# Six matmuls without a use in each batch of the channel attention

## The chip, the cores and the metric

The kernel runs on one core of a Trainium2 chip. The metric is the device time of one execution in microseconds (us), from the start of the program to its end; less is better.

## The reference

Four stages are added one after another to `x` (16 batches of 64 tokens with 256 channels): a gated attention, a mixture of experts, a channel attention and a gated MLP with four-bit weights. The change touches the third:

```python
def _L1_xattn_ref(q, k, v, gamma):
    # q = layernorm(x), k = v = ctx_2048, each (16, 64, 256)
    qh = q.reshape(B, 8, 8, 256); kh = k.reshape(B, 8, 8, 256); vh = v.reshape(B, 8, 8, 256)
    qk = jnp.einsum('bhdq,bhdl->bhql', qh, kh) * scale
    sm = jax.nn.softmax(qk, axis=-1)
    ret = jnp.einsum('bhql,bhdl->bhdq', sm, vh)
    return gamma * ret.reshape(B, Dv, Lq)
x = x + jnp.tanh(g_xattn[1]) * _L1_xattn_ref(...)
```

So in each of the 16 batches 8 heads attend from 256 channels to 256 channels, with only 8 numbers per head and channel in the product.

## The kernel before, in words

`build` (L1693 on) puts the four stages one behind the other. In `channel_attention` each batch passes over the engines like this. TensorE's orders are written out by hand in one loop over the batches, and semaphores tie the engines together.

- `replicate` (L1450): two matmuls of 128 rows and 128 columns against the constant `spread` lay a batch's rows (`split`, the normed x) and its context (`c_split`) out so that heads stand in strips of 32 rows. ScalarE copies the result to `qk_rows` (L1553).
- `row_scores` (L1465), four pairs of heads for a batch: four matmuls each that use 32 rows of the array. VectorE takes the maxima of a pair (L1620) into `context_mx`.
- `turn_maxima` (L1473): two transposes of the maxima; VectorE copies them to `mT` (L1626).
- `column_scores` (L1485, L1490), four pairs: two matmuls over 512 columns that subtract the maxima and four that add the scores, all on 32 rows. They wait for a free bank of three, which ScalarE's exponents (L1561, two for a pair) release.
- `weigh` (L1506): eight float32 matmuls, which the profile lists as sixteen, on strips of 32 output columns; called twice for a batch, with heads 0 to 3 and heads 4 to 7. They write columns 0 to 255 of the bank `OUT_BANK`. When the second is done VectorE takes the values out (L1630), inverts, scales and adds them to x.

The loop works one batch ahead. For batch b it runs, in this order: `replicate(b+2)`, row scores 1 of batch b+1, column scores 0 of batch b, row scores 2 of b+1, column scores 1 of b, the second weighing of batch b-1, row scores 3 of b+1, column scores 2 of b, `replicate(b+2)`, the first weighing of b, the turned maxima of b+1, row scores 0 of b+2, column scores 3 of b. Two weighings thus stand close together, and a long piece of the loop, from the turned maxima to the next weighing, holds none. Ahead of the loop `keep_busy` (L52) runs matmuls of the identity in the same bank `OUT_BANK`.

Of the kernel before, what the change touches and what calls it, by code (L numbers as in the profile page):

```python
# [26 lines left out]
BATCH, SEQ, HID = 16, 64, 256  # L27
# [21 lines left out]
def keep_busy(nc, k, bank, count):  # L49

    for _ in range(count):
        nc.tensor.matmul(k.ps[:, bank, :].rearrange("p (r n) -> p r n", r=4), k.ident[:],  # L52
                         k.ident[:].unsqueeze(1).broadcast_to([P, 4, P]), start=True, stop=True)
# [1318 lines left out]
def channel_attention(nc, k, a):  # L1372
# [5 lines left out]
    x, ident, vec, ps = k.x, k.ident, k.vec, k.ps  # L1378
    k.late_stack = ExitStack()
    k.ffn = FourBitWeights(nc, k, a, k.late_stack)  # L1380
    with ExitStack() as st:
# [8 lines left out]
        c_split, cT = k.context.split, k.context.turned  # L1390
        spread, minus, mx, vmask = k.context.spread, k.context.minus, k.context.mx, k.context.vmask
# [11 lines left out]
        A_BANK, B_BANK, OUT_BANK = 0, 4, 7  # L1403
# [5 lines left out]
        def a_use(b, what):  # L1409
            return (PAIRS + 1) * b + what  # L1410
# [15 lines left out]
        def cut(head):  # L1426
            group, j = divmod(head, C_GROUP)
            return group, slice(C_ROWS * j, C_ROWS * j + C_ROWS)

        @block.sync  # L1430
        def _(sp):

            k.ffn.load(sp, 0, 0)
            k.ffn.load(sp, 0, 1)

        @block.tensor
        def _(pe):
            mm = nc.tensor.matmul

            def replicate(b, group):  # L1440
                n = b_use["rows", b, group]
                if n >= 3:

                    pe.wait_ge(s["b_taken"], n - 2)
                if 2 <= b < 2 * FIRST_TILES and group == 0:
                    pe.wait_ge(s["h_low"], b // 2 * 2 + 2)
                elif b >= 2 * FIRST_TILES and group == 0:
                    pe.wait_ge(s["rest_low"], 2)
                for which, src in enumerate((split, c_split)):
                    last = mm(ps[:, B_BANK + n % 3, which * HID:which * HID + HID], spread[:, 2 * group + which, :], src[:, b, :],  # L1450
                              start=True, stop=True)
                last.then_inc(s["b_ready"], 1)

            def row_scores(b, pair):
                n = a_use(b, pair)
                if pair % 2 == 0:

                    pe.wait_ge(s["b_taken"], b_use["rows", b, pair // 2] + 1)
                if n >= 2:

                    pe.wait_ge(s["a_taken"], n - 1)
                for qt in range(CH):
                    for e in range(2):
                        group, rows = cut(2 * pair + e)
                        last = mm(ps[:, A_BANK + 2 * (n % 2) + e, qt * HID:qt * HID + HID], qk_rows[rows, b % 3, group, 0, qt * P:qt * P + P],  # L1465
                                  qk_rows[rows, b % 3, group, 1, :], start=True, stop=True)
                last.then_inc(s["a_ready"], 1)

            def turn_maxima(b):
                n = a_use(b, TURN)  # L1470
                pe.wait_ge(s["a_taken"], n)
                for qt in range(CH):
                    last = nc.tensor.transpose(ps[:, A_BANK + 2 * (n % 2), qt * P:qt * P + P], mx[:, qt, :], ident[:])  # L1473
                last.then_inc(s["a_ready"], 1)

            def column_scores(b, pair):
                n = b_use["head", b, 2 * pair]
                if pair == 0:

                    pe.wait_ge(s["a_taken"], a_use(b, TURN) + 1)  # L1480

                pe.wait_ge(s["b_taken"], n - 1)
                for e in range(2):
                    group, rows = cut(2 * pair + e)
                    mm(ps[:, B_BANK + (n + e) % 3, :].rearrange("p (c n) -> p c n", c=CH), minus[rows, group, :],  # L1485
                       mT[rows, b % 2, :].unsqueeze(1).broadcast_to([C_ROWS, CH, HID]), start=True, stop=False)
                for c in range(CH):
                    for e in range(2):
                        group, rows = cut(2 * pair + e)
                        last = mm(ps[:, B_BANK + (n + e) % 3, c * HID:c * HID + HID], qk_rows[rows, b % 3, group, 1, c * P:c * P + P],  # L1490
                                  qk_rows[rows, b % 3, group, 0, :], start=False, stop=(c == CH - 1))
                        if c == CH - 1:
                            last.then_inc(s["b_ready"], 1)

            def weigh(b, turn):

                pe.wait_ge(s["b_taken"], b_use["head", b, 4 * turn + 3] + 1)
                if turn == 0:
                    pe.wait_ge(s["values_set"], b + 1)
                    if b > 0:  # L1500

                        pe.wait_ge(s["out_taken"], b)
                for c in range(CH):
                    for quarter in range(4):
                        t, e = divmod(quarter, 2)
                        last = mm(ps[32 * quarter:32 * quarter + 32, OUT_BANK, 0:HID], vmask[:, b % 2, c, 2 * turn + t + 4 * e, :],  # L1506
                                  probs[:, 4 * turn + quarter, c * HID:c * HID + HID],
                                  start=(turn == 0 and c == 0), stop=(turn == 1 and c == CH - 1))
                last.then_inc(s["pv_done"], 1)

            keep_busy(nc, k, OUT_BANK, 5)
            pe.wait_ge(s["h_low"], 2)
            replicate(0, 0)
            replicate(0, 1)
            row_scores(0, 0)
            replicate(1, 0)
            row_scores(0, 1)
            replicate(1, 1)
            for pair in range(2, PAIRS):
                row_scores(0, pair)  # L1520
                keep_busy(nc, k, OUT_BANK, 1)
            turn_maxima(0)
            row_scores(1, 0)
            for b in range(BATCH):
                if b + 2 < BATCH:
                    replicate(b + 2, 0)
                if b + 1 < BATCH:
                    row_scores(b + 1, 1)
                column_scores(b, 0)
                if b + 1 < BATCH:  # L1530
                    row_scores(b + 1, 2)
                column_scores(b, 1)
                if b > 0:
                    weigh(b - 1, 1)
                if b + 1 < BATCH:
                    row_scores(b + 1, 3)
                column_scores(b, 2)
                if b + 2 < BATCH:
                    replicate(b + 2, 1)
                weigh(b, 0)  # L1540
                if b + 1 < BATCH:
                    turn_maxima(b + 1)
                if b + 2 < BATCH:
                    row_scores(b + 2, 0)
                column_scores(b, 3)
            weigh(BATCH - 1, 1)

        @block.scalar
# [240 lines left out]
```

## Time and profile before

| what | us |
|---|---|
| median of three runs | 1049.33 |
| lowest and highest of the three | 1041.99 and 1057.7 |
| the profiled execution, its own time | 1057.21 |
| span of the profiled execution, first to last instruction | 1055.4 |

The profiled execution lies close to the slowest of the three runs; 1.8 us of its time lie outside its span. "PE" is TensorE's matmuls, "PEld" its weight loads, DVE is VectorE, ACT ScalarE, POOL GpSimd. "PEclk" is the granted TensorE clock: 1.00 is 2.4 GHz, 0.50 is 1.2 GHz, and a figure between is a mean over a stretch that has some of both.

### The profile page before, as it was taken

What the parts mean: (1) busy time and instruction counts of PE and PEld (TensorE: products, weight loads), DVE (VectorE), ACT (ScalarE), POOL (GpSimd) and SP (SyncE); (2) the same over time, 40 slices, a digit from 0 to 9 for tenths busy, and PEclk for the clock granted to TensorE, in tenths of its full rate; (3) what the DMA queues carried; (4) which work ended last, traced back from release to release, by engine and by line L of the source; (5) the groups of instructions that cost most, each with busy time, mean ns of one, the idle gap of its engine ahead of it and who ended that gap; (6) DMA issues with size and microseconds to landing.
All of it is one profiled execution on the core that took longest, in us unless ns stands there. A gap on an engine that the chain in (4) does not pass through costs nothing. (4 is left out here: it accounts for less than half of the span.)

```text
span 1055.4 us, 18475 instructions
## 1 busy us (share of the span) xinstructions
PE 927.1 (88%) x6890; PEld 748.7 (71%) x6892; DVE 739.1 (70%) x1240; ACT 564.4 (53%) x1713; POOL 275.9 (26%) x413
## 2 busy tenths in 40 slices
PE   1679999999999999667999999988999996899997
PEld 1678888888888889545777777764555553577776
DVE  7778898988989897665544444456777668657653
ACT  5667787877788877314333333323455544333332
POOL 1133333344333334112322222203011013123130
PEclk9989999999999999887999999996676668999999
DMA  3101010110101000024111110001000000010001
GB/s 143 41 1 61 2 61 2 62 42 21 61 1 61 2 22 2 1 82 154 48 48 48 48 48 3 0 0 60 1 2 2 1 1 30 32 61 30 30 0 40
DMA packets 10929, 35.74 MB, mean 34 GB/s; under 512 B 1248, under 2 KB 5344, under 8 KB 8544
## 3 DMA queue, kind: packets, MB, share of 16 engines
q1 hardware_dynamic: 10704, 34.64, 9.3%
q8 instruction: 49, 0.80, 0.3%
q14 instruction: 32, 0.26, 0.1%
q10 hardware_dynamic: 144, 0.03, 0.0%
HBM read 33.62 MB, written 1.05 MB: 33 GB/s over the span
## 5 line engine op out<-in xcount | busy, mean ns | idle before, releaser
L223 PE MATMUL ps<-wt_hi,xq 128*128 128x256 f32 (+1 forms) x512 | 125.5, 281 | 20.8 <-DVE ctx_lo L727 15.0
L223 PE MATMUL ps<-wt_lo,xq 128*128 128x256 f32 (+1 forms) x512 | 125.2, 285 | 0.0
L223 PEld LDWEIGHTS ps<-wt_hi,xq 128*128 128x128 f32 x512 | 101.0, 197 | 23.8 <-DVE ctx_lo L727 15.4
L370 ACT ACTIVATE square<-ps 128x128 bf16<-128x128 f32 x384 | 100.9, 295 | 27.8 <-PE ps L223 27.8
L1561 ACT ACTIVATE ca_probs<-ps 128x512 f32<-128x512 f32 x128 | 69.5, 595 | 71.2 <-PE ps L1490 71.2
L223 PEld LDWEIGHTS ps<-wt_lo,xq 128*128 128x128 f32 x512 | 100.8, 197 | 0.0
L1138 POOL TENSOR_TENSOR moe_w_lo<-moe_w_all,moe_w_hi 128x384 fp32r<-128x384 f32 x48 | 52.8, 1133 | 141.6 <-ACT moe_w_hi L1241 141.6
L517 POOL TENSOR_TENSOR rstd<-rstd,half_neg 128x6 f32<-128x6 f32 x64 | 88.3, 1380 | 5.0
L370 ACT ACTIVATION_READ_ACCUMULATOR square<-ps 128x1 f32 x384 | 85.9, 226 | 0.0
L1620 DVE TENSOR_REDUCE context_mx<-ps 128x4 f32<-128x1024 f32 x64 | 76.9, 1223 | 12.0 <-PE ps L1465 11.3
L1305 DVE TENSOR_TENSOR moe_act_g<-moe_act_g,ps 128x512 f32<-128x512 f32 x48 | 33.1, 690 | 71.6 <-PE ps L1175 71.6
L1257 ACT CAST moe_in_hi<-moe_inner 128x512 fp32r<-128x512 f32 x48 | 29.8, 621 | 94.6 <-DVE moe_inner L1308 83.0
L391 ACT ACTIVATE kT<-ps,vec 128x128 f32<-128x128 f32 x128 | 51.7, 458 | 49.2 <-PE ps L235 49.2
L294 PE MATMUL ps<-wp_hi,catq 128*128 128x256 f32 x256 | 66.9, 299 | 11.7 <-DVE catq L101 11.7
L1175 PE MATMUL ps<-moe_hT_hi,moe_w_hi 128*128 128x512 f32 x192 | 76.9, 400 | 0.0
L1175 PE MATMUL ps<-moe_hT_hi,moe_w_lo 128*128 128x512 f32 x192 | 76.4, 398 | 0.0
L1175 PE MATMUL ps<-moe_hT_lo,moe_w_hi 128*128 128x512 f32 x192 | 76.2, 397 | 0.0
L522 POOL TENSOR_TENSOR probs<-probs,total 128x512 f32<-128x512 f32 x32 | 35.2, 1099 | 154.2 <-DVE total L632 154.2
L232 PE MATMUL ps<-ident,qn 128*128 128x128 f32 x256 | 42.4, 290 | 27.4 <-DVE qn L601 27.4
L597 DVE TENSOR_TENSOR qn<-ps,rstd 128x512 f32<-128x512 f32 x64 | 44.1, 689 | 30.5 <-POOL rstd L517 30.4
L294 PE MATMUL ps<-wp_lo,catq 128*128 128x256 f32 x256 | 65.2, 292 | 0.0
L294 PEld LDWEIGHTS ps<-wp_hi,catq 128*128 128x128 f32 x256 | 51.5, 201 | 14.9 <-DVE catq L101 14.9
(211 smaller groups left out, 2602.8 us busy)
## 6 DMA issues: line engine op xcount, KB each, us to landing
moe_w_all<-in_experts SPq DMA_DIRECT2D x8, 1152.0 KB, 5.3
w_in<-in_wt SPq DMA_DIRECT2D x8, 1024.0 KB, 5.9
wp_in<-in_wp SPq DMA_DIRECT2D x8, 512.0 KB, 3.6
ffn_codes<-in_codes SPq DMA_DIRECT2D x8, 384.0 KB, 3.1
ffn_w_scales<-in_code_scales SPq DMA_DIRECT2D x8, 384.0 KB, 3.7
x_rows<-in_x SPq DMA_DIRECT2D x2, 512.0 KB, 4.6
ctx_in<-in_ctxT SPq DMA_DIRECT2D x1, 1024.0 KB, 9.3
context_rows<-in_ctx SPq DMA_DIRECT2D x1, 1024.0 KB, 9.8
```

The source lines that it names most:

```text
L223: last = mm(ps[:, first + bank, col:col + width], left[:, c, tokens], w[:, c, wcol:wcol + width], start=(j == 0), stop=(j == len(steps) - 1))
L232: last = nc.tensor.transpose(ps[:, bank, j * P:j * P + P], qn[:, i % 2, j, :], ident[:])
L294: last = mm(ps[:, CAT_BANK + j, q * HID:q * HID + HID], catq[:, f // HPG, f % HPG, t * P:t * P + P], w[:, f, :], start=(n == 0), stop=(n = ...
L370: last = nc.scalar.activation(square[:, i % 2, j, :], ps[:, bank, (j % 4) * P:(j % 4) * P + P], ACT.Square, scale=float(HD) ** -0.5, accum ...
L391: last = nc.scalar.activation(kT[:, r, t * P:t * P + P], ps[:, PROJ + 2 * (i % 2) + 1, r * P:r * P + P], ACT.Identity, bias=vec[:, V_HLN + ...
L517: nc.gpsimd.tensor_tensor(rstd[:, i % 2, :], rstd[:, i % 2, :], k.half_neg[:, 0:6], ALU.pow).then_inc(s["rstd_ready"], 1)
L522: nc.gpsimd.tensor_tensor(probs[:, r], probs[:, r], total[:, r, :].unsqueeze(2).broadcast_to([P, 8, SEQ]), ALU.mult).then_inc(s["probs_rea ...
L597: nc.vector.tensor_tensor(qn[:, i % 2, 0:4, :], ps[:, bank, :].rearrange("p (h d) -> p h d", h=4), rstd[:, i % 2, 0:4].unsqueeze(2).broadc ...
L1138: last = nc.gpsimd.tensor_tensor(w_lo[:, b, cols], w_all[:, b, cols], w_hi[:, b, cols].bitcast(F32), ALU.subtract)
L1175: last = mm(ps[:, bank, :], w[:, b, col:col + P], h[:, c, tokens], start=(n == 0), stop=(n == len(steps) - 1))
L1561: nc.scalar.activation(probs[:, head, :], ps[:, B_BANK + n % 3, :], ACT.Exp, scale=float(C_DIM) ** -0.5).then_inc(s["b_taken"], 1)
L1620: nc.vector.tensor_reduce(dst, ps[:, bank:bank + 2, :].rearrange("p e (q l) -> p e q l", q=CH), AX.X, ALU.max).then_inc(s["a_taken"], 1)
```

## The change

TensorE gets a helper `spare()` with two matmuls of 128 rows, 128 columns and 256 columns of moving data. Their operands are constant by then (`spread`, and the context of batches 0 and 1), they write columns 256 to 511 of `OUT_BANK`, which nothing reads, and they neither wait for a semaphore nor raise one. It is called in each of the 16 passes of the loop at three places: ahead of column scores 0, ahead of column scores 1, and behind column scores 1.

```diff
+            def spare():
+
+                for b in range(2):
+                    mm(ps[:, OUT_BANK, HID:2 * HID], spread[:, 0, :], c_split[:, b, :], start=False, stop=False, skip_group_check=True)
+
...
                 if b + 1 < BATCH:
                     row_scores(b + 1, 1)
+                spare()
                 column_scores(b, 0)
                 if b + 1 < BATCH:
                     row_scores(b + 1, 2)
+                spare()
                 column_scores(b, 1)
+                spare()
                 if b > 0:
                     weigh(b - 1, 1)
```

TensorE's matmuls of one pass before, from the second `replicate` matmul's end up to the second weighing (L1465 row scores, L1485 and L1490 column scores, L1506 weighing):

```order
 L1465 MATMUL ps<-ca_qk_rows 128x256 x4
-L1485 MATMUL ps<-ca_mT,context_minus 128x512 x2
-L1490 MATMUL ps<-ca_qk_rows 128x256 x4
-L1465 MATMUL ps<-ca_qk_rows 128x256 x4
-L1485 MATMUL ps<-ca_mT,context_minus 128x512 x2
-L1490 MATMUL ps<-ca_qk_rows 128x256 x4
-L1506 MATMUL ps<-ca_probs,context_vmask 32x256 x8
```

And the same piece of the changed kernel (L1498 is the new helper, and the weighing's line is now L1511):

```order
+L1498 MATMUL ps<-context_split,context_spread 128x256 x2
+L1485 MATMUL ps<-ca_mT,context_minus 128x512 x2
+L1490 MATMUL ps<-ca_qk_rows 128x256 x4
+L1465 MATMUL ps<-ca_qk_rows 128x256 x4
+L1498 MATMUL ps<-context_split,context_spread 128x256 x2
+L1485 MATMUL ps<-ca_mT,context_minus 128x512 x2
+L1490 MATMUL ps<-ca_qk_rows 128x256 x4
+L1498 MATMUL ps<-context_split,context_spread 128x256 x2
+L1511 MATMUL ps<-ca_probs,context_vmask 32x256 x8
```

Nothing changes its place against anything else; three pairs of matmuls are put in between. The other engines run the same instructions in the same order.

## Rows read from the trace of the kernel before

**Rows 1.** The page: its first line, and the granted clock in 40 slices.

```profile
span 1055.4 us, 18475 instructions
PEclk9989999999999999887999999996676668999999
```

**Rows 2.** Windows: the loop of the channel attention, and the stage behind it.

```profile
core 0: us, PE busy (x) PEld busy (x) DVE busy (x) ACT busy (x) POOL busy (x), PEclk, DMA share, GB/s
727.93:886.70 158.77, 145.98 (x1225) 85.60 (x1223) 111.92 (x165) 84.27 (x157) 17.49 (x114) 0.70 0.01 1
886.70:1055.40 168.70, 148.00 (x619) 113.89 (x620) 99.19 (x138) 55.03 (x81) 41.55 (x35) 0.96 0.10 35
```

**Rows 3.** Windows from one batch's turned maxima to the next; first, last two, three between.

```profile
727.93:738.24 10.31, 9.06 (x58) 5.68 (x56) 5.23 (x5) 5.60 (x9) 0.00 (x0) 0.50 0.01 2
...
770.73:778.26 7.53, 6.70 (x82) 4.17 (x79) 5.99 (x9) 5.06 (x10) 1.16 (x8) 1.00 0.01 2
778.26:787.71 9.45, 8.94 (x82) 4.99 (x78) 7.70 (x13) 5.54 (x11) 1.16 (x8) 0.77 0.01 2
787.71:799.47 11.76, 11.53 (x82) 6.80 (x78) 7.18 (x10) 5.30 (x10) 1.16 (x8) 0.50 0.00 0
...
870.24:877.00 6.76, 5.90 (x78) 3.66 (x74) 5.96 (x9) 4.53 (x9) 1.16 (x8) 1.00 0.00 1
877.00:886.70 9.70, 7.05 (x80) 4.00 (x80) 8.02 (x23) 5.47 (x11) 1.20 (x2) 1.00 0.01 2
```

**Rows 4.** Windows: four stretches of the loop that end where the clock changes.

```profile
769.70:783.40 13.70, 12.36 (x145) 7.63 (x144) 12.06 (x19) 9.54 (x20) 1.16 (x8) 1.00 0.01 2
783.40:800.40 17.00, 16.77 (x120) 9.34 (x116) 9.98 (x17) 7.34 (x14) 2.32 (x16) 0.50 0.00 0
800.40:803.80 3.40, 2.58 (x28) 1.87 (x26) 3.37 (x5) 2.39 (x5) 0.00 (x0) 1.00 0.02 5
803.80:807.20 3.40, 3.40 (x30) 1.71 (x32) 1.13 (x2) 1.35 (x3) 0.56 (x5) 0.51 0.00 0
```

**Rows 5.** Timeline of TensorE in the batch at clock 1.00: start, us, instruction, idle before.

```profile
772.20 0.50 PE L1465 MATMUL ps<-ca_qk_rows 32*128 32x256 f32 x4
773.11 0.49 PE L1485 MATMUL ps<-ca_mT,context_minus 32*128 32x512 f32 x2 [0.41 <-ACT ca_probs L1561]
...
774.49 0.50 PE L1485 MATMUL ps<-ca_mT,context_minus 32*128 32x512 f32 x2 [0.42 <-ACT ca_probs L1561]
...
775.15 1.07 PE L1506 MATMUL ps<-ca_probs,context_vmask 128*32 128x256 f32 x16
...
776.83 0.39 PE L1450 MATMUL ps<-ca_split,context_spread 128*128 128x256 f32 x1
777.05 0.28 PE L1450 MATMUL ps<-context_split,context_spread 128*128 128x256 f32 x1
777.26 1.07 PE L1506 MATMUL ps<-ca_probs,context_vmask 128*32 128x256 f32 x16
```

**Rows 6.** Timeline of TensorE in the batch at clock 0.50.

```profile
789.49 0.58 PE L1450 MATMUL ps<-ca_split,context_spread 128*128 128x256 f32 x1
789.87 0.41 PE L1450 MATMUL ps<-context_split,context_spread 128*128 128x256 f32 x1
790.22 0.79 PE L1465 MATMUL ps<-ca_qk_rows 32*128 32x256 f32 x4
...
792.70 0.79 PE L1485 MATMUL ps<-ca_mT,context_minus 32*128 32x512 f32 x2 [0.23 <-ACT ca_probs L1561]
...
793.85 1.94 PE L1506 MATMUL ps<-ca_probs,context_vmask 128*32 128x256 f32 x16
```

**Rows 7.** Timeline of TensorE ahead of the loop: full-array matmuls in a row at clock 1.00.

```profile
719.64 0.28 PE L1450 MATMUL ps<-context_split,context_spread 128*128 128x256 f32 x1
719.76 0.28 PE L1450 MATMUL ps<-ca_split,context_spread 128*128 128x256 f32 x1
```

**Rows 8.** Timeline of TensorE: waits in the first pass, and in the last.

```profile
732.59 0.80 PE L1485 MATMUL ps<-ca_mT,context_minus 32*128 32x512 f32 x2 [1.00 <-ACT ca_probs L1561]
...
734.50 0.79 PE L1485 MATMUL ps<-ca_mT,context_minus 32*128 32x512 f32 x2 [0.25 <-ACT ca_probs L1561]
...
885.58 1.07 PE L1506 MATMUL ps<-ca_probs,context_vmask 128*32 128x256 f32 x16 [1.17 <-ACT ca_probs L1561]
```

## The prediction

> **What bounds the kernel now.** I read the page first: its line of granted clocks is 8 or 9 tenths nearly everywhere, but 6 or 7 in five of six slices near the end of the third quarter [rows 1]. The windows view puts them in the loop of the channel attention: 158.77 us at a mean clock of 0.70, against 0.96 in the stage behind it [rows 2]. TensorE is busy 145.98 us of those 158.77, the next engine (VectorE) 111.92. So the loop is bound by TensorE, and its clock counts in full.
>
> Then I cut the loop at each batch's turned maxima. The same 82 matmuls take 7.53 us at clock 1.00 and 11.76 us at 0.50; a batch with some of both takes 9.45 us [rows 3]. That is the price of the clock: up to 4.23 us a batch. From the first turned maxima (727.93) to those of batch 14 (870.24) the loop needs 142.31 us for 14 passes; the last 13 take (870.24 - 738.24)/13 = 10.15 us each. On the scale from 7.53 to 11.76 they are (10.15 - 7.53)/4.23 = 62% at the lower level.
>
> Last I looked at what TensorE does before the clock changes. It goes down to 0.50 at 783.4 and 803.8 [rows 4]. Both times the piece without a weighing has just passed: score matmuls on 32 rows of the array, with waits of about 0.4 us for ScalarE [rows 5]; the next weighing has just begun or is about to. The clock comes up at 769.7, 800.4 and 807.2, when replicate matmuls, a weighing and often the turned maxima have just run. It is the same in the other spells of the loop. So I read this: the piece without a weighing does too little to hold 2.4 GHz, and the change puts full-array matmuls (128*128) just there.
>
> By the Trainium skill ("TensorE: Matmul & The Clock Gate", table of what matters for a kernel, "avoid throughput drops mid-kernel") the clock drops when there are idle gaps of microseconds between bursts of matmuls. The trace does not agree: the gaps before the fall at 783.4 are no longer than about 0.4 us. By that rule the new matmuls would cure nothing and only cost: that is the second rival below.
>
> **The change, part by part.** Nothing is removed or moved, no wait is added; nobody waits for the new matmuls but what stands behind them on TensorE.
>
> - *Price of one pair at 1.00.* A pair of replicate matmuls has the same shape and tile: 776.83 to 777.26 is 0.43 us [rows 5]. In a row without a stop one takes 0.12 us [rows 7], a pair 0.24. I take 0.43, since each pair stands among matmuls with other weights, as the replicate pair does. Bounds 0.24 and 0.43.
> - *Price of one pair at 0.50.* 789.49 to 790.22, 0.73 us [rows 6]; twice the lower bound, 0.48, is the other end.
> - *Places 1 and 2 at 1.00* lie in front of two waits for ScalarE's exponents, 0.41 and 0.42 us [rows 5]. The pair fills them and is free to within 0.02 us. Without that cover each costs 0.43.
> - *Place 3 at 1.00* stands before a weighing that does not wait [rows 5]: 0.43 us. So a batch at 1.00 takes 7.53 + 0.43 = 7.96 us. VectorE has 5.99 and 7.70 us of work in neighbouring batches [rows 3] and stays below that on the mean.
> - *A batch at 0.50* has cover only at place 2, 0.23 us [rows 6]: 11.76 + 3 x 0.73 - 0.23 = 13.72 us, that is 1.96 us more.
> - *The first pass* (10.31 us, all at 0.50) has waits of 1.00 and 0.25 us at places 1 and 2 [rows 3, 8]: 0 + 0.48 + 0.73 = 1.21, so 11.52 us.
> - *Behind batch 14* the clock is 1.00 in both kernels, and the last weighing waits 1.17 us for ScalarE anyway [rows 3, 8]: at most 0.43 for the pass of batch 14. I take 0.4.
> - *The bank.* The pairs write the bank that VectorE reads (L1630), other columns of it. No row shows what that costs; between 0 and 0.43 us a batch (VectorE waiting out one pair). I take 0, since the read starts after the weighing, with no pair beside it at 1.00.
>
> *The sum.* The clock is low when the loop starts, as before, and the new pairs do not raise it: it must first meet a stretch of weighing and replicating at the right moment. I take the first pass at 0.50 and the second half and half, (13.72 + 7.96)/2 = 10.84 us, then twelve at 1.00: 12 x 7.96 = 95.5 us. Together 11.52 + 10.84 + 95.5 = 117.9 us against 142.3: 24.4 less. With 0.4 at the end the gain is 24.0 us. The profiled execution's 1057.2 would become 1033.2 (span 1031.4). It lies 7.9 us above the median; the excess I put down to clock spells elsewhere, such as slices 17 to 19 [rows 1], which this does not touch. From the median 1049.3 I get 1025.3 us, 2.3% less.
>
> **The rivals.**
>
> 1. *Stuck at 1.2 GHz (ends slower).* A pair takes 0.73 us at the lower level and so stretches the very batches that are slow. If the clock does not come up, a batch costs 13.72 us. With n such batches after the first and the rest at 7.96 the loop takes 11.52 + 13.72n + 7.96(13 - n) + 0.4 = 115.4 + 5.76n. It equals 142.3 at n = 4.7, is 2% slower (21 us) at 8.3, and with n = 13 the kernel takes 1049.3 + 48 = 1097 us. For it: before, the clock stayed low for 17.0 us at a stretch [rows 4], 1.4 batches; the new batches are longer and their mixture at the lower level no denser (matmul busy 11.53 of 11.76 us already [rows 3]). Against it: every spell before ended within about one and a half batches, by replicate, weighing and turning, which all remain. Before, the alignment between batches and clock changes moved on from spell to spell; if longer batches repeat at the same alignment, all 13 can miss. Runs would then differ much. Chance 0.19; 1051 to 1097, middle 1074.
> 2. *The pairs cost but do not hold the clock.* By the mix before, (0.62 x 1.96 + 0.38 x 0.43) = 1.38 us in each of 13 batches, with 1.2 and 0.4 at the ends 19.5: 1069 us. For it: the skill's rule above, and that the first pass stays at 0.50 throughout although identity matmuls run ahead of it. Against it: nothing else but the kind of matmul distinguishes stretches that hold the clock from those that lose it. Chance 0.13.
> 3. *It holds, but not always.* The clock falls two more times, as once three batches were 9.45, 11.76 and about 9.2 us. Each fall costs some 5 us: 1035 us. For it: one pair at 1.00 adds only 0.43 us of full-array work to a piece that lasts from 778.3 to 782.7. Chance 0.16.
>
> **How the numbers follow.** Forecast 0.52, rivals 0.19, 0.13, 0.16. The forecast's own range: 14 passes with only the first at 0.50 and pairs at 0.34 (between the two bounds) give 11.5 + 13 x 7.87 = 113.8, 28 less, 1021; a full second batch at 0.50 gives 1028. The three runs lie 7 to 8 us around their median, so a median of three can be off by some 4: 1017 is the low end. The high end takes in rivals 3 and 2 and the better half of 1: 1069. About 2% (21 us, 1028.3) is what a measurement of this kernel can tell from no change. Faster by more: most of the forecast, a little of rival 3, 0.49. Slower by more (over 1070): 0.17, from rival 1 and the upper side of 2. Within: 0.34.
>
> **What would show it.** In the changed kernel's profile: granted clock near 0.95 in the loop instead of 0.70; batches of about 8.0 us from turn to turn; the waits for ScalarE at places 1 and 2 gone, with the new line's pairs in their stead; each pair 0.43 us to the next matmul; a spell at 0.50 only at the loop's start. Wrong, if batches at 1.00 take over 8.3 us (cover misjudged), if the clock falls in the piece with the pairs (rival 2 or 3), or if a spell at 0.50 outlasts two batches (rival 1).

## The result and the profile after

| | before | changed |
|---|---|---|
| median of 20 executions, us | 1055.84 | 1052.12 |
| lowest and highest, us | 1041.05, 1060.15 | 1031.50, 1107.77 |
| profiled execution, its own time and span, us | 1057.21, 1055.4 | 1091.61, 1089.8 |
| mean granted clock of the profiled span | 0.921 | 0.886 |

The comparison of the two gives 0.9877 (95% interval 0.9834 to 0.992), so 1.2% less; it leaves out the executions that lie more than 1.5% above the fastest of their kernel. In the changed kernel that is where the story is: they are ten of the 20, and the medians of all 20 differ by 0.4% only. With the runs called same_again and third_sample, which are the changed kernel once more, there are 36 executions, and they lie in three groups with nothing between them: 18 from 1031.5 to 1041.3 us, 10 from 1062.7 to 1068.8, and 8 from 1091.6 to 1107.8. Over all 36 the median is 1052.0. The kernel before spreads from 1041 to 1062 us in all its runs, without such gaps.

The profile after fell into the third group. The first line of its page and the granted clock in 40 slices, to be read against [rows 1]:

```profile
span 1089.8 us, 18669 instructions
PEclk8789999999999998888999999975555587899999
```

Where there were sixes there are now fives. The windows view, from turned maxima to turned maxima, in the columns of [rows 3]; last, the whole spell at the lower level:

```profile
core 0: us, PE busy (x) PEld busy (x) DVE busy (x) ACT busy (x) POOL busy (x), PEclk, DMA share, GB/s
728.65:740.06 11.41, 11.41 (x64) 7.27 (x62) 5.33 (x5) 5.60 (x9) 0.00 (x0) 0.50 0.01 1
740.06:753.80 13.74, 13.74 (x88) 8.24 (x84) 10.13 (x11) 5.30 (x10) 1.21 (x8) 0.50 0.00 1
753.80:767.55 13.75, 13.75 (x88) 8.25 (x85) 7.17 (x10) 5.30 (x10) 1.15 (x8) 0.50 0.00 1
...
863.78:877.52 13.74, 13.74 (x88) 8.24 (x84) 7.17 (x10) 5.30 (x10) 1.15 (x8) 0.50 0.00 0
877.52:886.30 8.78, 8.76 (x88) 5.51 (x85) 6.36 (x9) 5.07 (x10) 1.15 (x8) 0.89 0.01 2
886.30:894.27 7.97, 7.97 (x88) 5.08 (x84) 6.37 (x10) 5.30 (x11) 1.15 (x8) 1.00 0.01 2
894.27:902.42 8.15, 8.15 (x89) 5.11 (x85) 7.09 (x12) 5.29 (x11) 1.15 (x8) 1.00 0.00 0
...
722.40:879.40 157.00, 157.00 (x933) 93.66 (x931) 84.43 (x113) 59.60 (x111) 12.96 (x81) 0.50 0.00 1
```

TensorE is busy in every microsecond of 157 us and its clock stays at 1.2 GHz. Behind the first pass, ten follow each other at 13.74 or 13.75 us. In the next the clock comes up (8.78 us), and two passes of 7.97 and 8.15 us follow. From the first turned maxima to those of batch 14 the loop takes 902.42 - 728.65 = 173.8 us against 142.3 before: 31.5 of the 34.4 us that the profiled execution is slower. Of the rest 0.7 us had been lost before the loop (it starts at 728.65, not 727.93), and the remaining 2.2 come behind batch 14.

TensorE's timeline of one low pass, as in [rows 6] (L1498 is the new pair; the weighing is L1511 here):

```profile
838.79 0.79 PE L1465 MATMUL ps<-ca_qk_rows 32*128 32x256 f32 x4
839.51 0.80 PE L1498 MATMUL ps<-context_split,context_spread 128*128 128x256 f32 x2
840.24 0.79 PE L1485 MATMUL ps<-ca_mT,context_minus 32*128 32x512 f32 x2
...
841.81 0.80 PE L1498 MATMUL ps<-context_split,context_spread 128*128 128x256 f32 x2
842.54 0.79 PE L1485 MATMUL ps<-ca_mT,context_minus 32*128 32x512 f32 x2
...
843.69 0.80 PE L1498 MATMUL ps<-context_split,context_spread 128*128 128x256 f32 x2
844.41 1.94 PE L1511 MATMUL ps<-ca_probs,context_vmask 128*32 128x256 f32 x16
```

Each pair takes 0.72 or 0.73 us to the next matmul. And of a pass at 2.4 GHz, as in [rows 5]:

```profile
887.77 0.50 PE L1465 MATMUL ps<-ca_qk_rows 32*128 32x256 f32 x4
888.20 0.51 PE L1498 MATMUL ps<-context_split,context_spread 128*128 128x256 f32 x2
888.67 0.50 PE L1485 MATMUL ps<-ca_mT,context_minus 32*128 32x512 f32 x2
...
889.58 0.50 PE L1498 MATMUL ps<-context_split,context_spread 128*128 128x256 f32 x2
890.06 0.50 PE L1485 MATMUL ps<-ca_mT,context_minus 32*128 32x512 f32 x2
...
890.73 0.50 PE L1498 MATMUL ps<-context_split,context_spread 128*128 128x256 f32 x2
891.16 1.07 PE L1511 MATMUL ps<-ca_probs,context_vmask 128*32 128x256 f32 x16
```

The waits of 0.41 and 0.42 us for ScalarE are gone, filled by pairs of 0.47 and 0.48 us, and the third pair adds its 0.43 us in front of the weighing. This is a pass of 7.97 us.

### The profile page after: what moved, and what is told of

It is laid out like the page before. It is cut to its first block and busy times, and to the rows that moved or that the text cites. A ratio compares the mean times of both kernels' runs of the same rounds, so it can differ in the third digit from the quotient of the medians.

```text
span 1089.8 us, 18669 instructions
## 1 busy us (share of the span) xinstructions
PE 974.2 (89%) x6988; PEld 779.4 (72%) x6988; DVE 739.9 (68%) x1240; ACT 563.7 (52%) x1713; POOL 275.6 (25%) x413
```

## The experiments

The theories, as the expectations name them. A: the pairs hold the higher clock once it is there, but a low pass keeps in step with the moments at which the clock can change, so a low spell can last. B: the pairs only cost. C: any matmul in the waits would do. D: the third pair is needed. E: the more work at the low level, the longer it stays low. F: the start decides everything.

**The changed kernel again: same_again and third_sample.** No edit.

> The changed kernel once more, to see more executions and, if the profile falls on one, an execution that runs well. Theory A (the pairs hold the higher clock once it is there, but a pass at the lower level takes 13.75 us and repeats at nearly the same place against the moments at which the clock can change, so that a low spell can last for many passes): executions lie in clusters, some at 1031 to 1041 us and some at 1063 to 1108; passes at clock 1.00 take 7.97 us, with no fall inside the loop. Theory B (the pairs only cost, the clock moves as before): all executions near 1070 us, the clock goes up and down within the loop at passes of 8 to 13.7 us.

> The changed kernel a third time, for a profile of an execution that runs well (both profiles so far fell on executions near 1100 us). If the profile falls on one near 1032 to 1041: one low spell at the loop's start, passes of 7.97 and 8.15 us, and, as in the run called kick, a short fall of the clock in about one pass of four, 9.6 to 9.7 us. If it falls on the middle cluster (1063 to 1069): a low spell of 6 or 7 passes of 13.75 us, then the same.

Eight executions of the first: 1032.1, 1033.1, 1033.8, 1062.7, 1065.4, 1066.1, 1100.2, 1101.4 us. Eight of the second: five from 1031.8 to 1034.2, then 1066.7, 1067.7 and 1093.6. The groups are those of the first 20, so theory B, which has no groups, falls. Both profiled executions belong to the third group, with low spells that run through the first 13 and 12 passes. Behind the first pass of 11.40 us they are again of 13.74 and 13.75 us each. TensorE was busy throughout; the whole spell of same_again, and that of third_sample:

```profile
721.00:905.20 184.20, 184.20 (x1099) 109.92 (x1097) 98.28 (x133) 70.04 (x131) 15.74 (x98) 0.50 0.00 1
720.40:891.00 170.60, 170.60 (x1017) 101.75 (x1013) 90.95 (x122) 64.82 (x121) 14.55 (x90) 0.50 0.00 1
```

The pass at 1.00 that follows in third_sample is of 8.16 us; the one of batch 14, which has less to do (6.76 us before), takes 7.21 us in both.

The end of the three spells says more. The clock came up at 879.4, 905.3 and 891.0 us, which is each time 1.9 us behind the turned maxima of that pass (877.52, 903.38 and 889.19), though it was the 12th pass in one, the 14th in another and the 13th in the third. TensorE does the same work in the passes before it, and they agree to 0.01 us. So its work does not set that pass apart; when it came may, as theory A has it.

Neither the middle group nor the good one was ever profiled.

**Without the third pair: two_places.**

```diff
                 column_scores(b, 1)
-                spare()
                 if b > 0:
                     weigh(b - 1, 1)
```

> The third pair of each pass is left out, the two that stand in front of waits stay. Theory A: a pass at the lower level takes 11.76 + 0.73 + 0.50 = 13.0 us instead of 13.75 and so moves against the moments of change from pass to pass; low spells end within 3 to 5 passes, a pass at 1.00 takes 7.53 to 7.6 us; executions at 1025 to 1050 us, none over 1070, if two pairs still hold the clock. Theory D (the third pair is needed to hold the clock): the clock falls as before, executions near 1060 us. Theory B: 1055.8 plus 13 times about 0.75, near 1065 us.

Median 1031.38 us, lowest 1029.52, highest 1037.3 (6 executions); ratio 0.9825 (0.9775 to 0.9875). The windows of its first seven passes:

```profile
728.46:738.13 9.67, 9.02 (x61) 5.61 (x59) 5.14 (x5) 5.61 (x9) 0.00 (x0) 0.68 0.01 2
738.13:749.03 10.90, 9.37 (x86) 5.51 (x82) 9.84 (x11) 5.30 (x10) 1.22 (x8) 0.81 0.00 1
749.03:756.70 7.67, 7.67 (x87) 4.87 (x83) 6.00 (x9) 5.07 (x10) 1.16 (x8) 0.98 0.01 2
756.70:764.42 7.72, 7.72 (x87) 4.80 (x83) 7.09 (x12) 5.30 (x11) 1.16 (x8) 1.00 0.01 3
764.42:771.96 7.54, 7.54 (x87) 4.76 (x83) 6.37 (x10) 5.30 (x11) 1.16 (x8) 1.00 0.00 0
771.96:781.22 9.26, 9.26 (x86) 5.53 (x82) 7.51 (x13) 5.50 (x11) 1.16 (x8) 0.82 0.01 2
781.22:788.75 7.53, 7.53 (x86) 4.77 (x83) 6.08 (x9) 5.10 (x11) 1.16 (x8) 1.00 0.01 2
```

Every second pass at 1.00 takes 7.53 or 7.54 us, what it took without any pair [rows 3]: there the two covered pairs are free. The passes between take 7.72 us, of which more below. The clock was still going up and down in the first two passes. Behind them it fell once, and came back within the pass (9.26 us); the other passes up to batch 14 are at 1.00. There was no long spell. So D falls: the third pair is not needed. Against "the pairs hold the clock" without a limit stand those falls.

**Six narrow matmuls instead: narrow.**

```diff
-mm(ps[:, OUT_BANK, HID:2 * HID], spread[:, 0, :], c_split[:, b, :], ...
+mm(ps[:, OUT_BANK, HID:2 * HID], spread[0:32, 0, :], c_split[0:32, b, :], ...
```

> The six matmuls of a pass use rows 0 to 31 of the array only; as many, as long, at the same places. If what holds the clock is how much of the array works (theory A): the clock falls in the loop as in the kernel before, no execution near 1032, all within 1055 to 1100. If it is that the waits are filled with any matmul (theory C): the same clusters as the changed kernel, the fast one at 1031 to 1041 us.

Median 1042.63 us (1034.89 to 1046.94, 12 executions), ratio 0.9909 (0.9876 to 0.9942). Neither expectation is met. The timeline of TensorE at 1.00:

```profile
748.51 0.39 PE L1465 MATMUL ps<-ca_qk_rows 32*128 32x256 f32 x2
748.52 0.38 PE L1498 MATMUL ps<-context_split,context_spread 32*128 32x256 f32 x1
748.73 0.28 PE L1465 MATMUL ps<-ca_qk_rows 32*128 32x256 f32 x2
748.75 0.28 PE L1498 MATMUL ps<-context_split,context_spread 32*128 32x256 f32 x1
749.41 0.50 PE L1485 MATMUL ps<-ca_mT,context_minus 32*128 32x512 f32 x2 [0.39 <-ACT ca_probs L1569]
```

At the first and the third place the narrow matmuls start 0.01 to 0.02 us behind the score matmuls, which sit on other rows of the array, and run beside them; the wait for ScalarE at the first place stays, 0.39 us. At the second place both use rows 0 to 31; there the narrow ones run behind the scores and leave 0.22 us of the wait. So they were not "as long" as the full ones, as I had said: they cost the pass nothing, and the passes at 1.00 stay at 7.53 and 7.54 us. Nor do they fill the waits, so theory C was not put to the test. The Trainium skill ("TensorE: Matmul & The Clock Gate", Part 3 on packing small matmuls) says that matmuls on different row groups run at the same time; the trace agrees. Six such matmuls gain 0.9%, two full ones (first_place, below) 1.2% and four full ones 1.75% (two_places), so the clock is helped by narrow work too, and by four full ones more than by six narrow ones (their intervals do not touch; that of first_place overlaps with both). The full ones differ in two things, the part of the array that they use and the waits that they fill, and no run tells these apart. None of the 12 executions lies above 1046.94 us: with pairs that cost nothing there was no long spell.

**A start at 2.4 GHz: kick.** On top of the change:

```diff
-            keep_busy(nc, k, OUT_BANK, 5)
+            keep_busy(nc, k, OUT_BANK, 8)
...
                 spare()
+                if b == 0:
+                    keep_busy(nc, k, OUT_BANK, 1)
                 column_scores(b, 0)
```

> The changed kernel with three more full-array matmuls of the identity ahead of the first replicate matmuls (8 instead of 5, where TensorE stood idle for 2.8 us) and one more in the first pass in front of column scores 0 (where it waited 1.0 us): the clock is meant to be at 1.00 when the loop starts. Theory A: then no execution has a long low spell; 15 passes of 8.0 us; the median 1020 to 1030 us and the spread under 10 us. Theory B: no gain beyond the first passes, median as for the changed kernel.

Median 1032.82 us (1031.19 to 1036.81, 6 executions), ratio 0.9831 (0.9781 to 0.9881). The spread is 5.6 us, and none of the six lies in the upper groups, where the changed kernel has 18 of 36 (if nothing had changed, six would all miss them once in 64 times). The median is 3 us higher than the top of what I expected, and the windows of its passes say why. Three at the start, and a run of five further on:

```profile
725.47:733.36 7.89, 7.87 (x65) 4.92 (x65) 5.23 (x5) 5.37 (x9) 0.00 (x0) 1.00 0.01 2
733.36:743.82 10.46, 8.97 (x89) 5.33 (x85) 9.80 (x11) 5.53 (x11) 1.21 (x8) 0.91 0.00 1
743.82:752.44 8.62, 8.62 (x89) 5.51 (x85) 6.12 (x9) 5.07 (x10) 1.15 (x8) 0.91 0.01 2
...
768.56:778.25 9.69, 9.69 (x89) 5.75 (x85) 7.08 (x12) 5.29 (x11) 1.15 (x8) 0.82 0.01 2
778.25:786.23 7.98, 7.98 (x89) 5.08 (x85) 6.38 (x10) 5.32 (x11) 1.15 (x8) 1.00 0.01 2
786.23:794.38 8.15, 8.15 (x88) 5.08 (x84) 7.09 (x12) 5.28 (x11) 1.15 (x8) 1.00 0.00 1
794.38:802.37 7.99, 7.99 (x89) 5.07 (x85) 6.39 (x10) 5.31 (x11) 1.15 (x8) 1.00 0.01 2
802.37:812.00 9.63, 9.63 (x89) 5.69 (x85) 7.10 (x12) 5.29 (x11) 1.15 (x8) 0.82 0.01 2
```

Two things stand here. In every fourth pass the clock falls and comes back, at 9.63 to 9.69 us instead of 8.15, some 1.5 us each. And the second pass takes 10.46 us although its clock is 0.91: VectorE has 9.80 us of work in it, among it the two splits of the remaining rows (L867) of 1.75 us each. The 14 passes up to batch 14 take 120.3 us here.

**The same start without the pairs: kick_alone.**

> The kernel before with the same four extra matmuls of the identity as in the run called kick, and no pairs. If the pairs are what holds the clock in the loop (theory A), this loses the clock within the first pass or two and then goes up and down as before: the gain is the first pass at most, about 3 us, median 1047 to 1055. If the start decides everything (theory F), the clock stays up and the median is 1025 to 1035 us.

Median 1049.66 us (1037.93 to 1056.67, 12 executions) against 1056.76 of the kernel before, measured beside it; ratio 0.9934 (0.9884 to 0.9983). The clock was lost in the first pass, and the next two were 11.15 and 10.41 us:

```profile
726.57:735.36 8.79, 7.89 (x59) 4.39 (x59) 5.24 (x5) 5.61 (x9) 0.00 (x0) 0.86 0.01 2
735.36:746.51 11.15, 10.01 (x83) 5.49 (x79) 9.92 (x11) 5.30 (x10) 1.21 (x8) 0.65 0.00 1
746.51:756.92 10.41, 9.61 (x82) 5.43 (x79) 7.08 (x10) 5.30 (x10) 1.15 (x8) 0.67 0.01 2
```

F falls: a start at 2.4 GHz does not hold without the pairs. Of the 1.7% that kick gains, and the 2.5% of two_places_kick below, 0.7% comes with this alone.

**Only the third pair: third_place.** `spare()` is called behind column scores 1 only.

> Only the pair at the third place stays. A pass takes 7.53 + 0.43 = 7.96 us at 1.00 and 11.76 + 0.73 = 12.49 at 0.50. If the clock is held by full-array work anywhere in the piece without a weighing, this holds it about a third as well: falls in most passes, median 1050 to 1060 us, no clusters. If one pair is enough, 1032 to 1040 us.

Median 1066.03 us (1060.09 to 1069.65, 6 executions), ratio 1.0106 (1.0052 to 1.0159): 1% slower. Two of its windows, a pass with both levels and one at the lower:

```profile
748.14:759.40 11.26, 10.44 (x84) 5.94 (x80) 7.08 (x10) 5.30 (x10) 1.15 (x8) 0.65 0.01 1
759.40:771.89 12.49, 12.26 (x84) 7.32 (x80) 6.94 (x10) 5.30 (x10) 1.15 (x8) 0.50 0.01 2
```

The low pass is the 11.76 + 0.73 = 12.49 us of the expectation. Mean clock over the 14 passes: 0.66, as in the kernel before. This pair costs its time at both levels and holds nothing by itself.

**Only the first pair: first_place.** `spare()` is called ahead of column scores 0 only.

> Only the pair ahead of column scores 0 stays. It is free at 1.00 (7.53 us) and costs 0.73 us at 0.50 (12.5 us). If the two covered pairs hold the clock together and one does not: falls every second or third pass, median 1042 to 1052 us, no clusters. If the first pair alone does it: 1031 us as with two places.

Median 1038.39 us (1035.12 to 1044.91, 6 executions), ratio 0.9881 (0.9829 to 0.9933); mean clock over the 14 passes 0.82. It is better than expected: two matmuls in a pass bring as much as the change's six in this comparison, and none of the six executions lies in its upper groups.

**One matmul more, and one fewer, at the third place: seven and five.** `spare` takes a count here; `spare(1)` in five.

```diff
-                spare()
+                spare(3)
                 if b > 0:
                     weigh(b - 1, 1)
```

> The changed kernel with three matmuls instead of two at the third place, so one more in each pass. If long low spells come from a pass that keeps in step with the moments of change (theory A), a longer low pass ends them: passes of 13.75 + 0.36 = 14.1 us at 0.50, spells over after at most 8 passes, no execution over about 1080; the executions in the middle cluster spread out. If they come from the amount of extra work at the low level (theory E: the more work, the longer it stays low), spells become longer: at least as many executions over 1090 us as before, the highest near 1113. At 1.00 a pass takes 7.97 + 0.12 to 0.21 = 8.1 to 8.2 us in either case.

> The changed kernel with one matmul instead of two at the third place, so one fewer in each pass: 13.75 - 0.36 = 13.4 us at 0.50, 7.97 - 0.2 = 7.75 at 1.00. Theory A (keeping in step): a pass at 0.50 now moves the other way against the moments of change, by more than the 13.75 us pass did; no spell of 150 us, no execution over about 1080, some near 1045 to 1065. Theory E (work at the low level alone): the same three clusters as the changed kernel, the highest near 1095 instead of 1101.

Seven: 12 executions, seven from 1035.2 to 1049.0, four from 1057.0 to 1057.9 and one at 1165.2; median 1045.75. The profiled execution is the fastest. A window of it:

```profile
738.40:857.80 119.40, 117.44 (x1219) 74.93 (x1219) 99.53 (x151) 76.15 (x144) 17.07 (x114) 1.00 0.01 2
```

The clock stays at 1.00 for 119.4 us without a break, in passes of 8.09 and 8.29 us. The upper group lies 16 us above the median of the good ones (1041.0), where the two of the changed kernel lie 33 and 64 above theirs (1033.5). That is what A expects of a low pass that is longer and so falls out of step sooner; E expects at least as many above 1090 us as before, which would be two or three of 12. The one at 1165.2 us fits neither: A had named nothing over 1080, E a highest of 1113. Its mean clock over the whole span is 0.733, where 0.873 was the lowest in the changed kernel; even 14 low passes of 14.1 us would add only some 14 x 5.9 = 83 us to 1035. So something outside the loop took part, and I cannot say what. Five: 1033.4, 1034.3, 1035.5, 1035.9, 1041.9, 1067.6, 1068.2; median 1035.86. None of seven is above 1080, where 8 of 36 were; with so few that decides little. And the two upper ones lie where the middle group of the changed kernel does, not at 1045 to 1065 as A had it. The two runs do not decide between A and E.

**Two pairs and the start: two_places_kick, and mixed_kick with a narrow third pair.**

> The two pairs in front of waits, and the four extra matmuls at the start: the version that should be best. Theory A: the first two passes go from 9.67 and 10.90 us (as in the run with two places) to about 8 and 7.7, the rest as there: 4 to 5 us less than 1031.4, median 1026 to 1028 us, spread under 10 us. If starting high does not help, 1031 us.

> The run called kick with the third pair on rows 0 to 31 of the array only; pairs of that kind ran beside their neighbours at no cost to the pass in the run called narrow. If the third pair pays for itself when it is free: passes at 1.00 of 7.54 to 7.75 us and fewer falls than with two places; median 1024 to 1027 us. If it adds nothing to the two pairs: 1027 us, as two_places_kick.

Median 1026.97 us (1025.87 to 1029.26), ratio 0.9747 (0.9699 to 0.9794), and 1028.06 us (1024.56 to 1029.25), ratio 0.9763 (0.9719 to 0.9806), six executions each. The first has the lowest median, and it is the only run whose whole interval lies below 0.98; the narrow pair adds nothing that can be told from it. None of the first's six executions is as slow as the fastest of two_places (1029.52). The windows of its first, second and fourth pass:

```profile
726.39:735.39 9.00, 8.53 (x62) 4.88 (x62) 5.24 (x5) 5.61 (x9) 0.00 (x0) 0.86 0.01 2
735.39:746.27 10.88, 9.36 (x86) 5.47 (x82) 9.81 (x11) 5.30 (x10) 1.21 (x8) 0.81 0.00 1
...
753.96:761.68 7.72, 7.72 (x87) 4.79 (x83) 7.09 (x12) 5.29 (x11) 1.16 (x8) 1.00 0.01 3
```

The first two passes did not get to 8 and 7.7 us as I had expected. Of the 2.7 us between the profiled executions of two_places and this run, 2.1 lie before the loop, which starts at 726.39 instead of 728.46 us; the 14 passes take 113.1 us instead of 113.8. That the new start won those 2.1 us is not shown: without it the loop started anywhere from 725.71 (narrow) to 729.23 us (five).

Of the profiled executions, the 14 passes and their mean clock side by side. One execution stands for each kernel here, and it is not always a usual one, so its own time and the median of its run stand beside:

| kernel | 14 passes, us | clock | this execution, us | median, us |
|---|---|---|---|---|
| before | 142.3 | 0.66 | 1057.21 | 1055.84 |
| changed (third group) | 173.8 | 0.57 | 1091.61 | 1052.12 |
| same_again (third group) | 185.1 | 0.52 | 1100.21 | 1064.03 |
| third_sample (third group) | 179.5 | 0.54 | 1093.56 | 1033.87 |
| third_place | 151.7 | 0.66 | 1069.65 | 1066.03 |
| first_place | 125.2 | 0.82 | 1039.08 | 1038.39 |
| kick_alone | 123.4 | 0.83 | 1040.37 | 1049.66 |
| five | 123.8 | 0.89 | 1041.93 | 1035.86 |
| narrow | 119.4 | 0.85 | 1034.89 | 1042.63 |
| kick | 120.3 | 0.94 | 1033.25 | 1032.82 |
| seven | 118.1 | 0.97 | 1035.17 | 1045.75 |
| mixed_kick | 115.8 | 0.91 | 1029.25 | 1028.06 |
| two_places | 113.8 | 0.94 | 1029.52 | 1031.38 |
| two_places_kick | 113.1 | 0.95 | 1026.84 | 1026.97 |

kick_alone warns of reading too much into one row: without any pair in the loop its profiled execution, one of its fast ones, has a clock of 0.83. narrow's is its fastest of 12.

## Why the prediction was right or wrong

**What bounds the loop: right.** The clock is its price. With two covered pairs the same work at clock 0.94 takes 113.8 us instead of 142.3.

**The prices: right.** A pair at 0.50 was put at 0.73 us and took 0.72 to 0.73. A low pass was put at 13.72 us and took 13.75; one at 1.00 at 7.96 and took 7.97; the first pass at 11.52 and took 11.41. Places 1 and 2 are free at 1.00 as said in every second pass (7.53 us in two_places). One thing was missed: the passes between take 8.15 us, not 7.97, and 7.72 rather than 7.53 in two_places. Those are the passes in which VectorE also turns back and adds (7.09 us busy). The trace of the changed kernel shows where that counts: VectorE begins to take maxima at 895.99, 1.72 us behind the turned maxima, instead of 0.91 us (887.21), and row scores 2, which need the first of these banks back, start 0.36 us behind the matmuls before them instead of 0.24. Without pairs the same delay goes into the second wait for ScalarE, which in such a pass of kick_alone is 0.17 us, where [rows 5] have 0.42, and that pass stays at 7.54. A pair in that place takes the slack. No run tried it. The bank term, which I had put at nothing, was nothing: VectorE's read of `OUT_BANK` takes 0.45 us in both kernels.

**What failed: the sum's "I take the first pass at 0.50 and the second half and half", with twelve passes at 1.00 behind them.** The number of low passes is not about one and a half. The three profiled executions had 11, 13 and 12 low passes, the first among them, and 8 of 36 executions lie in their group. A low pass costs 13.75 - 7.97 = 5.78 us more than a high one. By that, an estimate from times alone, the third group, 58 to 74 us above the median of the good one, has 10 to 13 more, and the middle group of ten, some 33 us above, has 5 or 6 more. That is rival 1, with its mechanism and its price: I had written 1051 to 1097 us and "if longer batches repeat at the same alignment, all 13 can miss". I gave it 0.19, and it had 8 of 36 executions as the profiles show, and 18 if the middle group is of the same kind. The argument that I set against it, that every spell before had ended within one and a half batches, was taken from passes of 11.76 us, whose length the change alters.

Why a spell lasts is not settled. That it is not the pairs' failing to hold the clock once it is up shows in kick, which has all the change's pairs and a clock of 0.94, and none of whose six executions is above 1036.8 us. That the passes keep in step with the moments at which the clock can change (A) has for it that alike passes went by until one, at the same place in the pass in all three profiles, brought the clock up. Leaving out the third pair (no execution of 6 above 1037.3) fits A, but also E, since it takes away length and work at the lower level at once. Seven and five were to tell these apart and did not. So A is the better argued reading, and it is not shown.

**The start from the median: a second fault.** I put the profiled execution's 7.9 us above the median down to spells elsewhere and subtracted the gain from 1049.3. Over 20 executions the median of before is 1055.84, so the profiled one was a usual one, and the three had fallen low. From 1055.8 the same gain of 24.0 gives 1031.8 us. The 18 good executions lie at 1031.5 to 1041.3, 13 of them below 1034.2. By their times the gain of a good execution was rightly sized, though none was profiled; the median of all is 1052, as half of them are not good.

**The second rival** (the pairs only cost, and the clock goes up and down as before) is ruled out for the good group by its times and for the third by its profiles. The middle group lies at 1062.7 to 1068.8 us, just below this rival's 1069, and has no profile; that its low passes come in one spell is not shown. **The third** (the clock holds, but not always) is likely part of the good executions, if kick stands for them: a fall in every fourth pass, at 1.5 us and not 5.

By the Trainium skill's rule on idle gaps (the page "TensorE: Matmul & The Clock Gate", table of what matters for a kernel) the pairs could only cost. They did more: in two_places the mean clock of 14 passes was 0.94 instead of 0.66, and the median 1031.38 us against 1051.58 of the kernel before, measured beside it. And in the changed kernel the clock stayed at 0.50 through 157.0 us in which TensorE was busy for 157.00. Neither the absence of gaps nor matmuls back to back brought it up.

## What to carry to other kernels

A matmul without a use that stands in front of a wait can be free while the clock is high and cost its full time while it is low, when the wait is gone. So put it only where a wait covers it, and check its price at the lower level, not only at the higher. Two covered pairs in a pass did better than three pairs, one of them uncovered, and six executions with them had no long tail. When the granted clock goes up and down in a loop, treat the number of low passes as a distribution, which a change of the loop can widen as well as shift. Take more than three executions before you name a median to start from, and do not read a kernel's clock from one profiled execution.

## What the runs showed of the hardware

- TensorE's clock stayed at 1.2 GHz for 157.0, 184.2 and 170.6 us while it was busy without a break, with passes of 13.74 and 13.75 us. With a pass of one matmul more, it held 2.4 GHz for 119.4 us in the profiled execution.
- In all three of these spells the clock came up 1.9 us behind the turned maxima, after 11, 13 and 12 low passes.
- Score matmuls on 32 rows and narrow matmuls on 32 other rows start 0.01 to 0.02 us apart and take no time from each other: six narrow ones in a pass, two of them in a wait, leave it at 7.53 us.
- Those six narrow matmuls brought the kernel to 0.9909 of its time (0.9876 to 0.9942), and one full-array pair brought it to 0.9881 (0.9829 to 0.9933) at the first place and to 1.0106 (1.0052 to 1.0159) at the third.
